# Expert weights loaded once, their half sums and differences formed by GpSimd ahead of the first scatter

## What is computed

```python
xn = layernorm(x)
# branch s: a filter of the spectrum, then 24 bits of a latent, corrected and projected back
x1 = ifft(fft(xn) * filt(D)).real            # D from xn.flat[0:1024]
bits = (sigmoid(x1 @ W_el + b_el) > 0.5)
s = x1 + golay_correct(bits) @ W_le + b_le
# branch g: two of eight experts for each token
probs = softmax(xn @ router_w.T)             # 8 numbers for each token
topk_vals, topk_idx = top_k(probs, 2)
topk_w = topk_vals / (topk_vals.sum(-1) + 1e-6)
expert_out = einsum('nh,eho->eno', xn, expert_weights)
g = silu(sum over both of (chosen expert_out + remap_bias) * topk_w)
out = x + s * g
```

## Time and profile before

| | us |
|---|---|
| median of three runs | 1313.28 |
| lowest and highest | 1309.83, 1315.61 |
| profiled execution | 1313.39 |
| its span | 1311.1 |
| PE busy | 1125.4 |
| DVE busy | 1098.4 |
| ACT busy | 481.4 |
| POOL busy | 928.0 |

### The profile page before, as it was taken

The page is one execution under the profiler, slowest core; times in us unless marked ns, Lnnn a source line. Parts: engine busy times, 40 slices in busy tenths (PEclk is TensorE's granted clock), DMA queues, the critical chain, the costliest instruction groups (busy, mean ns, idle before and its releaser), DMA issues. The chain is left out here.

```text
span 1311.1 us, 26949 instructions
## 1 busy us (share of the span) xinstructions
PE 1125.4 (86%) x6039; PEld 598.3 (46%) x6040; DVE 1098.4 (84%) x2699; ACT 481.4 (37%) x1123; POOL 928.0 (71%) x903
## 2 busy tenths in 40 slices
PE   3858788760086789999999999999999999999996
PEld 3534455430032235555555555555555555555553
DVE  6389898899166658898999999899999899999985
ACT  3736655540033323333333333333333333333331
POOL 2047777686566637787888887788888778888874
PEclk9889999885599889999999999999999999999999
DMA  9837889710189966666666666666666666666664
GB/s 343 315 133 185 202 169 222 163 34 16 41 202 214 211 154 158 174 173 171 175 172 173 174 176 171 169 172 172 173 175 177 171 171 177 173 175 171 171 170 108
DMA packets 278573, 224.33 MB, mean 171 GB/s; under 512 B 212831, under 2 KB 212831, under 8 KB 278418
## 3 DMA queue, kind: packets, MB, share of 16 engines
q1 hardware_dynamic: 230162, 140.04, 44.7%
q0 software_dynamic: 31872, 79.79, 20.6%
q10 hardware_dynamic: 16512, 4.19, 1.7%
HBM read 131.75 MB, written 47.12 MB: 136 GB/s over the span
## 5 line engine op out<-in xcount | busy, mean ns | idle before, releaser
L1356 PE MATMUL banks<-w_hi,arena 128*128 (+1 forms) x1136 | 434.6, 383 | 44.9 <-DMA arena<-arena 43.9
L1357 PE MATMUL banks<-w_lo,arena 128*128 (+1 forms) x1136 | 434.0, 382 | 0.0
L1358 PE MATMUL banks<-w_hi,arena 128*128 (+1 forms) x1136 | 433.6, 382 | 0.0
L723 ACT ACTIVATE arena<-xbuf,inf 128x512 f16<-128x512 f32 x156 | 112.6, 722 | 573.8 <-DVE xbuf L1162 573.8
L534 POOL DMA_INDIRECT xbuf<-in_L_attn_x,gidx x156 | 181.3, 1162 | 96.4 <-issue 65.2
L536 POOL DMA_INDIRECT inf<-token_info,gidx x156 | 192.2, 1232 | 54.1 <-issue 52.8
L1356 PEld LDWEIGHTS banks<-w_hi,arena 128*128 128x128 f16 x1136 | 111.6, 98 | 183.1 <-issue 58.8
L573 POOL TENSOR_TENSOR xbuf<-xbuf 128x512 f32<-128x512 f32 x128 | 162.1, 1267 | 40.2 <-DVE xbuf L1226 32.5
L511 POOL DMA_INDIRECT pair_tokens<-tok,slot x128 | 128.2, 1002 | 70.6 <-issue 44.0
L1358 PEld LDWEIGHTS banks<-w_hi,arena 128*128 128x128 f16 x1136 | 111.9, 99 | 134.1 <-issue 4.4
L540 POOL DMA_INDIRECT out<-xbuf,sidx x128 | 141.6, 1107 | 40.9 <-issue 40.6
(11 more groups left out here) (277 smaller groups left out, 1730.4 us busy)
## 6 DMA issues: line engine op xcount, KB each, us to landing
xbuf<-in_L_attn_x SPq DMA_DIRECT2D x32, 1024.0 KB, 11.4
arena<-extra_sums SPq DMA_DIRECT2D x128, 256.0 KB, 2.7
arena<-in_L_ffn_expert_weights SPq DMA_DIRECT2D x16, 1024.0 KB, 9.2
extra_sums<-arena SPq DMA_DIRECT2D x28, 256.0 KB, 3.6
token_info<-info ACTq DMA_DIRECT2D x8, 512.0 KB, 8.4
xbuf<-in_L_attn_x,gidx POOLq DMA_INDIRECT x156, 3.6
inf<-token_info,gidx POOLq DMA_INDIRECT x156, 2.8
arena<-arena SPq DMA_TRANSPOSE x156, 4.0
```

The source lines that it names most:

```text
L723: nc.scalar.activation(hi4[ring(i, k)], uv2[:, b], ACT.Copy, scale=inf2[:, k, 1:2]).then_inc(hi_ready, 1)
L1356: mm(ps, hi[:, c], wh, start=(c == 0), stop=False)
L1357: mm(ps, hi[:, c], wl, start=False, stop=False)
L1358: end = mm(ps, lo[:, c], wh, start=False, stop=(c == C - 1))
```

## The change

Each expert is loaded once. The eight loads go through a ring of two buffers (LH = 2); both the norm and the butterfly read the same copy, and the load of expert `e` waits until norm and butterfly of expert `e` - 2 are done. POOL forms the butterflies of experts 0 to 6, then the maximum over the partitions, then the butterfly of expert 7, then waits for the table's fill, and after that only scatters. The half sums of all eight experts are kept in fp32 in the memory in which `w_lo` will be written; the ring `raw` moves behind `diff`. The norms of experts 3 to 7 are put at the steps (0,1), (0,2), (0,3), (1,0) and (1,2) of ScalarE, its root and VectorE's `scales()` at step (1,3). `high` and `low_sums` of expert `i` - 2 stand in round `i` (2 to 7), those of experts 6 and 7 behind the rounds. The table is filled by three stores from the constants (of which SP's wait `ld_cst` is the first condition), and no longer from `far`; ScalarE doesn't wait for the fill any more.

```diff
-    LH = 4
+    LH = 2
+    FILLS = 3
-        raw = arena[:, 0:8192].rearrange("p (s c e) -> p s c e", s=LH, c=C)
         diff = arena[:, 0:NE * CH * E].rearrange("p (s c e) -> p s c e", s=NE, c=CH)
-        prep = arena[:, 8192:8192 + C * E].rearrange("p (c e) -> p c e", c=C)
-        quart = arena[:, 10240:10240 + 2 * CH * E].rearrange("p (s c e) -> p s c e", s=2, c=CH)
+        raw = arena[:, NE * CH * E:NE * CH * E + LH * C * E].rearrange("p (s c e) -> p s c e", s=LH, c=C)
+        quart = w_lo[:, :, :, :].rearrange("p s c e -> p (s c e)").bitcast(F32).rearrange("p (s c e) -> p s c e", s=NE, c=CH)
...
-            def load_for_norm(e):
+            def load_expert(e):
+                after(sp, wpm_ready, e - LH + 1)
                 after(sp, norm_ready, e - LH + 1)
                 sp.dma_start(raw[:, e % LH], experts[e].rearrange("(c p) o -> p c o", p=P)).then_inc(ld_w[e % LH], 16)
-
-            def load_expert(e):
-                after(sp, wpm_ready, e)
-                sp.dma_start(prep, expert_rows[:, bass.ds(e, 1)].rearrange("p o c n -> p (o c) n")).then_inc(ld_prep, 16)
-            load_for_norm(0)
-            load_for_norm(1)
+            load_expert(0)
+            load_expert(1)
             load(0, 0)
-            sp.wait_ge(far_ready, 1)
-            sp.dma_start(pair_tokens.rearrange("(p r) c -> p (r c)", p=P), far).then_inc(far_stored, 16)
             load(0, 1)
-            for e in range(2, NE):
-                load_for_norm(e)
-                if e < U:
-                    load(0, e)
-            load_expert(0)
+            load_expert(2)
+            load(0, 2)
+            load(0, 3)
+            load_expert(3)
+            sp.wait_ge(ld_cst, 16)
+            table = pair_tokens.rearrange("(p h r) c -> p h (r c)", p=P, h=FILLS)
+            for h in range(FILLS):
+                sp.dma_start(table[:, h], cst[:, 0:TROWS // FILLS].bitcast(I32)).then_inc(far_stored, 16)
             for k in range(U):
                 load(1, k)
-            load_expert(1)
+                load_expert(U + k)
             with sp.Fori(2, R) as i:
                 for k in range(U):
                     load(i, k)
-                load_expert(i)
...
-            def halves(e, buf=0):
-                h2 = quart[:, buf]
-                if not isinstance(e, int):
-                    pool.wait_ge(wsum_ready, e)
-                pool.wait_ge(ld_prep, 16 * (e + 1))
-                pool.sem_inc(prep_seen, 1)
-                G.tensor_tensor(diff[:, bass.ds(e, 1)].rearrange("p o c n -> p (o c) n"), prep[:, 0:CH], prep[:, CH:C],
-                                ALU.subtract).then_inc(wdiff_ready, 1)
+            def halves(e):
+                w = raw[:, e % LH]
+                pool.wait_ge(ld_w[e % LH], 16 * (e // LH + 1))
+                G.tensor_tensor(diff[:, e], w[:, 0:CH], w[:, CH:C], ALU.subtract).then_inc(wdiff_ready, 1)
                 pool.wait_ge(wdiff_ready, e + 1)
+                pool.wait_ge(norm_ready, e + 1)
...
-            halves(0)
-            halves(1, 1)
-            pool.wait_ge(far_stored, 16)
-            with pool.Fori(0, R - 2) as i:
+            for e in range(NE - 1):
+                halves(e)
+            pool.wait_ge(norm_ready, NE)
+            G.partition_all_reduce(norm_all[:, :], norm2[:, :], P, RMAX).then_inc(norm_red, 1)
+            halves(NE - 1)
+            pool.wait_ge(far_stored, 16 * FILLS)
+            with pool.Fori(0, R - 1) as i:
                 scatter(i)
-                halves(i + 2)
-            scatter(R - 2)
             scatter(R - 1, 1)
...
+            NORM_AT = [(0, 1), (0, 2), (0, 3), (1, 0), (1, 2)]
...
-                if later and k == 3:
-                    act.wait_ge(wpm_ready, i + 1)
-                    act.wait_ge(wsc_ready, i)
                 latT_copy(i, k)
...
+                if not head and k == 3:
+                    act.wait_ge(wpm_ready, NE)
+                    act.wait_ge(wsc_ready, i)
+                    high(i - 2, wsc[:, 0])
...
                 if k == 3:
+                    if isinstance(i, int) and i == 1:
+                        scales()
                     if later:
                         weigh(i - 1, beside=newton_steps(i))
```

63 lines of the change are left out of this document (25 added, 38 removed).

## The result

The changed kernel takes 1323.02 us (median of 9 runs, 1319.3 to 1328.14), the kernel before 1310.23 us in as many runs (1302.17 to 1315.61). The ratio is 1.0099, with a 95% interval of 1.0076 to 1.0121. The profiled execution took 1327.79 us (span 1325.6), 14.4 us more than the one before.

What follows compares the result with a forecast made beforehand. Scatters and their drain were taken to bound the token-sorting rounds. +8.1 to the second list, -10.6 in four loops and -2.3 in the last loop gave -4.8: 1308.6 us, range 1298 to 1322 (8 in 10).

Steps and rivals of the forecast that it cites:

- Term 1: Setup: butterflies beside VectorE's setup chain stretch it by 9.8 us (0 to 12); ScalarE's first copies come 4.5 later.
- Term 2: First choice of experts: starts at 67.5, takes 24 us, ends at 91.5 instead of 93.33; last square done at 96.9.
- Term 3: New chain from last square through maximum, 7.0 us idle and last butterfly: first scatter at 112.0, 10.6 us later.
- Term 4: First burst 22.1 us and its drain 6.0: second list's cast at 140.1 instead of 132.0, +8.1 us.
- Term 5: Four loops: the removed expert load takes 2.7 us off each drain, period 29.2, -10.6 us in all.
- rival E: Four loops: drain as long as before, made by token loads; +8.3 us, 1321.7 us in all; chance 0.25.
- Term 6: Last loop: falls from 27.33 to 25.0 us, with 2.6 gone from VectorE; -2.3 us.
- Term 7: What stays: main phase 0; in the tail, butterfly 7's going worth 0.2 us and left out, moved expert work under idle.
- B: Rounds: butterflies, not the load, slow the drain; it falls to 6, loops 27.2, 1300.6 us in all; chance 0.22.
- D: Setup: it isn't stretched, so the first scatter comes 4.5 us earlier, 1304.1 us in all; chance 0.13.
- F: SP's queue: butterfly waits hold expert and token loads; no more than 3 us, counted with rival E, no chance of its own.

Runs made afterwards that it cites:

- a_hold: Changed kernel with butterflies held until VectorE's setup chain is done, third square moved to step (0,0), two token loads ahead of expert 2's load: 1298.96 us, ratio 1.0008.
- a_last: Changed kernel with the maximum over the partitions put behind the butterfly of expert 7 instead of ahead of it: 1315.37 us, ratio 1.0141.
- a_addload: Changed kernel with one more 1 MB load in each round from 2 on, issued right after the burst: 1321.2 us, against 1308.85 for the changed kernel.
- a_tinyx: Changed kernel with the token loads of rounds 2 to 7 cut to 16 numbers of one tile in four: 1293.07 us in one execution.
- b_nobfly: Kernel before with the six butterflies in the rounds cut to 8 columns, loads kept: 1286.89 us in one execution.
- a_fix: a_hold with the square of expert 7 at step (1,1) and the maximum behind the last butterfly: 1295.55 us, ratio 0.9983 to the kernel before.
- a_fixslots: a_fix with token and slot lists of their own for each round: 1285.21 us, ratio 0.9907 to the kernel before.
- a_best2: a_fixslots plus a one-column GpSimd addition behind the table's gathers, run again in another group: 1275.76 us, ratio 0.9837 to the kernel before.
- a_best: a_fixslots plus a one-column GpSimd addition behind the table's gathers, in the group with before at 1350.99: 1358.69 us, ratio 1.0054.

## Why the prediction was wrong, step by step

The forecast was 1308.6 us, 4.8 below, range 1298 to 1322; it came out at 1323.02, 12.8 above the median of before. The path that it followed was the right one, and two of its terms had wrong sizes.

**Term 1, the setup: the first step that failed.** It took 9.8 us for what butterflies do to VectorE's setup chain, between 0 and 12; the chain's end came 18.3 later (48.94 against 30.63), 17.4 of them beside the work of GpSimd from 20.8 on. The measure was taken from the choice of experts, which lay beside two butterflies and lost 9.7 us. But the setup lay beside nearly continuous work of GpSimd from 20.8 to 44.7, 24 us and not 14.8, since GpSimd never had to wait there, and it has copies, casts and instructions with a scalar, which were stretched even more than those with two inputs (2.34 us for 0.17 at 21.25; 1.24 for 0.29 at 24.28). And the term looked at ScalarE's squares as what held the first copies; they were held by TensorE, whose turning stands in its program behind the product with wcat. Copies 13.7 us later instead of 4.5. a_hold, with the chain undisturbed, gives back what this term had missed.

The Trainium skill ("SBUF — State Buffer", Who interferes with whom) says that copies, casts and instructions with a scalar can enter a two-port mode, and that the engine which comes second is then fully blocked. The rows at 21.25 and 34.80 agree: 2.34 and 2.31 us, where the same instructions took 0.17 and 0.28. The prediction named the rule, and held only the two-input instruction against it.

**Term 2.** The choice started at 79.55 instead of 67.5. 9.2 us of that are the first copies (50.5 instead of 41.3). The rest lies in VectorE's six small instructions ahead of the choice, which took 5.3 us beside a butterfly (74.22 to 79.51) and 1.2 before (60.85 to 62.02); the sum had no term for them. The choice itself took 21.5 us (79.55 to 101.04) instead of 24.

**Term 3, the new chain, was right**: from the end of the last square (106.16) to the first scatter 15.5 us, forecast 15.1, with a gap of 7.03 and a butterfly of 7.6. It began 9.3 us late. What it had not seen: a second gap ahead of the maximum, seen in a_last and no cost here, where a wait of 11.88 us stands in its place.

**Term 4** was right: 22.1 and 6 us were forecast for burst and drain after the first scatter, and it took 28.4 to the cast. Terms 1 to 4 together: +18.0 instead of +8.1.

**Term 5, the four loops: the second step that failed.** It gave the removed load 2.65 us in each, 10.6 in all; the loops became shorter by 0.66 (31.81 to 31.15), 2.65 in all. The price may have been near (1.0 to 1.9 in a_addload), the place was wrong: "the whole 2.7 off the drain" took for granted that the load lay in the drain, while its issue stood behind burst and butterfly, at 161. The mechanism is that of rival E: the drain is made by the token loads (a_tinyx). Its time, 1321.7, is 1.3 us from the median, but by luck: it was +8.3 on a profiled execution of 1313.39, and the profiled execution now is +14.4. It had the setup at 9.8, which is too little, and nothing for the loops; and the median of before fell from 1313.28 in three runs to 1310.23 in nine. That the loops failed apart from the setup is seen in a_hold: its first scatter (111.90) and its second list (138.84) are where terms 1 to 4 had put them (112.0 and 140.1), and its ratio is 1.0008, where the forecast is 0.9964.

**Term 6 was right** (24.8 for 25.0; VectorE's 2.6 us in a loop are gone, 99.88 / 4 = 25.0 busy). **Term 7**: nothing in the main phase, as said; the tail took 1.3 us more; its last drain alone is 1.9 longer (5.69 against 3.83).

**Rivals.** B, that the butterflies and not the load make the drain long, falls: its loops of 27.2 weren't seen with the butterflies out of the rounds (31.15 in the changed kernel, 29.7 in b_nobfly); that they add a little to the drain isn't excluded. D, a setup that isn't stretched, was the opposite of what happened. F, that butterfly waits hold SP's queue, was counted under 3 us: a wait of 22.38 us on GpSimd for the fourth square did delay loads 5 to 7 and the token loads behind them. But the first list didn't wait for them: between 49 and 108 us no row of TensorE, ScalarE or VectorE waits for a token load; ScalarE waited 0.7 and 2.7 us for expert loads (squares at 77.33 and 85.02) and then stood 5.68 us for VectorE's choice, and VectorE had no idle time from 79.55 to the list.

The range ended at 1322, just under the result. The setup term's upper bound was drawn from one stretch of two butterflies and not from the program order, which let GpSimd run on without a wait. With 18.3 us in place of 9.8, rival E would have stood at 1321.7 + 8.5 = 1330.2, and the result inside the range.

## What to carry to other kernels

Work that is moved off the loop's path isn't free where it goes: price it against the program of the engine that it disturbs, instruction by instruction, for as long as the mover can run without a wait, and look for what the disturbed chain releases on other engines. A transfer that is taken away shortens a wait only if it was in flight during that wait: compare the times of issue with the start and the end of the drain before giving it a price. And GpSimd's change from one kind of instruction to the other and back costs about 7 us twice here; the return is paid by the next instruction of the first kind, however late, so put a small one under a wait.

## What the runs showed of the hardware

- GpSimd stands idle, with no releaser in the profile, between tensor instructions and the reduction over partitions in both directions: 7.39 us ahead of the reduction when a butterfly preceded it (a_last), 7.03 behind it, and 7.0 to 7.8 us at the first tensor instruction even when some 250 us of scatters and gathers lay between (a_last, a_fix, a_fixslots). Scatters right behind the reduction have none of it (0.22 us in a_last). That this is a change of set-up is the reading; that it is paid once, by the next tensor instruction, is shown by a_best2, where a one-column addition took 7.09 us of idle and the later one had none.
- VectorE's copies and scalar instructions of 0.2 to 0.4 us took 2.3 to 2.5 us, five of six of them, beside GpSimd's 128 x 1024 instructions; a chain of 10.6 us (20.07 to 30.63) grew to 27.9 us (21.01 to 48.94).
- Loads of 1 MB take more of the DMA engines' time in rounds with scatters of 4 bytes and stores of 0.5 MB: 387 GB/s at a share of 1.05 for loads alone, 126 GB/s at 0.61 in the changed kernel's loops. The scatters' own packets take 1.5% in either case, yet the last of a burst has landed about 10 us after its issue with token loads in flight (loops of the changed kernel) and 3.8 to 5.7 us after it in the tail.
- The same kernel had medians from 1296.51 to 1350.99 us in the groups of this case, three of them with the same chip number; and the same edit (a_best, a_best2) gained 1.6 per cent in one group and lost 0.5 in another.
